# An up projection over the whole TensorE array, zero-padded table products, and bias rows in free strips

## The reference

```
x = x + L0(x)      # per-entry low-rank weight:  x @ (U V)
x = x + L1(x)      # styled linear layer with demodulation and clamp
# L2, an adapter; dg, db, ug, ub come from the entry's condition (256 -> 64 -> 256 features)
down = einsum('bsd,bdh->bsh', x, down_project * dg + db)
up   = einsum('bsh,bhd->bsd', relu(down), up_project * ug[b] + ub[b])
x = x + (up + x)
# L3: layer norms of x with gain and shift looked up by class ids, then a two-layer net
h = LN(LN(x, pw[id]), cp[id]);  t = LN(x, tm[id]);  s = LN(x, ms[id])
m, n, r = x + per-entry rows;   cat = [w0 h, w1 t, w2 m, w3 n, w4 r, w5 s]
x = x + LN(silu(cat @ int_W1 + int_b1) @ int_W2 + int_b2)
```

## Time and profile before

| | |
|---|---|
| median of three runs | 538.83 us (535.41 to 541.04) |
| span of the profiled execution, first to last instruction | 530.8 us |
| median less that span | 8.0 us |
| mean granted TensorE clock | 0.988 of full speed |
| busy: TensorE, VectorE, ScalarE, GpSimd | 497.0, 406.6, 326.3, 390.5 us |

### The profile page before, as it was taken

How to read it: one execution, slowest core, us unless ns; L and a number is a source line. 1 busy time by engine, 2 the same in 40 slices (tenths; PEclk the granted TensorE clock), 3 DMA queues, 4 the chain that set the end, 5 groups by cost and what they waited for, 6 DMA issues and landing times.

```text
span 530.8 us, 9969 instructions
## 1 busy us (share of the span) xinstructions
PE 497.0 (94%) x3454; PEld 352.4 (66%) x3454; DVE 406.6 (77%) x707; ACT 326.3 (61%) x622; POOL 390.5 (74%) x367
## 2 busy tenths in 40 slices
PE   2987988989999999999999999999999999999993
PEld 2953654757777676767676767677676767687682
DVE  1858877758888787879787878788787978786753
ACT  4574647346666576756765757567575767656822
POOL 6468798788787879697877787787878693777321
PEclk9999998999999999999999999999999999999997
DMA  8887714625252262708070716244352613104102
GB/s 297 244 297 201 198 40 101 159 81 123 81 120 84 48 194 39 202 5 237 0 219 23 190 52 162 80 114 128 78 165 41 203 33 89 48 17 145 40 2 79
DMA packets 35639, 61.85 MB, mean 117 GB/s; under 512 B 6002, under 2 KB 18062, under 8 KB 35229
## 3 DMA queue, kind: packets, MB, share of 16 engines
q1 hardware_dynamic: 29404, 44.03, 30.2%
q0 software_dynamic: 5344, 16.87, 11.0%
q10 hardware_dynamic: 864, 0.61, 0.4%
HBM read 52.63 MB, written 8.87 MB: 116 GB/s over the span
## 4 chain that ended last, share of the span: by engine, by line
PE 78%; DVE 10%; issue 4%; DMA 4%; ACT 2%; POOL 1%; DVEq 0%; SPq 0%; POOLq 0%; ACTq 0%
PE ps_c L906 13%; PE ps_c L908 11%; PE ps_c L907 11%; PE ps_d L952 10%; PE ps_a L982 6%; PE ps_d L966 5%; PE ps_a L994 3%; PE ps_a L1000 3%; PE ps_b L1000 3%; DMA set_wdec<-in_nets_rows 3%; PE ps_b L939 3%; DVE tm_t_l L1439 3%; DMA set_wdec<-in_W_dec 1%; PE ps_a L488 1%; PE ps_b L923 1%
## 5 line engine op out<-in xcount | busy, mean ns | idle before, releaser
L1509 POOL DMA_INDIRECT pw_rows<-in_pw,gidx x64 | 63.4, 990 | 17.9 <-issue 17.4
L952 PE MATMUL ps_d<-xm_t,l_w 128*128 128x512 f32 x128 | 58.9, 603 | 1.2 <-POOL xm_t L1518 0.8
L1208 ACT ACTIVATE h<-h,nb_h,rstd_h 128x256 f32<-128x256 f32 x64 | 33.3, 591 | 33.8 <-POOL nb_h L1533 33.8
L1518 POOL TENSOR_TENSOR xm_t<-x_t,style 128x1024 f32<-128x1024 f32 x16 | 30.5, 1905 | 26.4 <-DVE x_t L1343 26.4
L1548 POOL TENSOR_TENSOR h<-xhat,pw_rows 128x1024 f32<-128x1024 f32 x16 | 37.9, 2369 | 7.6 <-ACT xhat L1208 7.1
L952 PEld LDWEIGHTS ps_d<-xm_t,l_w 128*128 128x128 f32 x128 | 23.1, 190 | 25.9 <-issue 24.2
L1567 POOL TENSOR_TENSOR w_up<-up_rep,ugub 128x1024 f32<-128x1024 f32 x16 | 37.9, 2367 | 2.2 <-issue 2.0
L1553 POOL TENSOR_TENSOR h<-h,pw_rows 128x1024 f32<-128x1024 f32 x16 | 38.3, 2392 | 1.3
L1569 POOL TENSOR_TENSOR w_up<-w_up,ugub 128x1024 f32<-128x1024 f32 x16 | 38.2, 2387 | 1.3
L906 PE MATMUL ps_b<-w_h,act_t_l 128*128 128x256 f32 x128 | 37.7, 295 | 0.4 <-DVE act_t_l L1452 0.4
L1239 ACT ACTIVATE tm_t_h<-ps_a 128x1024 fp32r<-128x1024 f32 x16 | 16.4, 1027 | 34.8 <-DVE ps_a L1415 34.8
(11 more groups left out here) (247 smaller groups left out, 1527.0 us busy)
## 6 DMA issues: line engine op xcount, KB each, us to landing
ugub<-ugub_scratch SPq DMA_DIRECT2D x32, 512.0 KB
x_t<-in_x_t SPq DMA_DIRECT2D x16, 512.0 KB
out<-y_out SPq DMA_DIRECT2D x15, 512.0 KB
set_wdec<-in_W_dec SPq DMA_DIRECT2D x2, 1920.0 KB, 9.7
set_wdec<-in_int_W SPq DMA_DIRECT2D x1, 1536.0 KB, 10.6
set_wdec<-in_nets_rows SPq DMA_DIRECT2D x1, 1152.0 KB, 13.6
pw_rows<-in_pw,gidx POOLq DMA_INDIRECT x64
set_wdec<-in_nets_W SPq DMA_DIRECT2D x1, 768.0 KB, 4.9
```

The lines of the kernel that those rows point to most:

```text
L952: m = eng.matmul(ps_l1[:, o, :], l1_w[:, k, o * P:(o + 1) * P], xm_t[:, k, :], start=k == 0, stop=k == KB - 1)
L1208: m = eng.activation(out[:, j, :], src[:, j, :], ACT.Identity, bias=nb[k][:, j:j + 1], scale=rstd[k][:, j:j + 1])
L1509: eng.indirect_dma_start(pw_rows[c.ring][:, j, :], None, t["pw"], bass.IndirectOffsetOnAxis(ap=gidx[c.ring][:, j:j + 1], axis=0)).then_inc ...
```

## The change

- The up projection becomes eight matmuls of 128 weight rows and 128 columns. `act_dn` is [128, 4, 2, 64] and zero off its two diagonal blocks (rows of e hold columns of e), so that one full-array product gives both entries. `act_relu` writes the two blocks in two instructions, `v_x3sum` adds in one.
- The ms scale product and the shift product use all 128 rows of tables and one-hot, with zeros where nothing belongs; their two matmuls are therefore full-array ones. The shift table's two blocks lie side by side in 256 columns, its DMA per chunk is one instead of two.
- The bias rows of the second layer move to partitions 32 and 96, next to the tm product at 0 and 64.
- Seven tiles are zeroed at the start on VectorE instead of one, and their first users wait for that; `act_shift` copies the shift table in one instruction instead of two and the bias rows in two instead of one.

```
-        shift = [sb(f"shift{r}", [P, P], BF16) for r in range(2)]
+        shift = [sb(f"shift{r}", [P, D], BF16) for r in range(2)]
-        act_dn = sb("act_dn", [P, CT * S])
+        act_dn = sb("act_dn", [P, CT, 2, S])
-        pads = (ubias_p,)
+        pads = (ubias_p[:, :], act_dn[:, :, :, :], onehot[0][:, :], onehot[1][:, :], shift[0][:, :], shift[1][:, :], gain_tab[:, 2 * D:3 * D],)
...
 def load_entry
-                for lo in (0, STRIP):
-                    eng.dma_start(onehot[n][lo + CLS:lo + CLS + BRW, :], t["entry_rows"]).then_inc(d_oh, 16)
+                eng.dma_start(onehot[n][CLS:CLS + BRW, :], t["entry_rows"]).then_inc(d_oh, 16)
...
 def v_classes
-            for k in range(KB):
-                m = eng.tensor_copy(shift[0][k * STRIP:k * STRIP + CLS, :], src[:, k * P:(k + 1) * P])
-            m.then_inc(v_cls, 1)
+            eng.tensor_copy(shift[0][0:CLS, :], src).then_inc(v_cls, 1)
...
 def act_shift
-            for k in range(KB):
-                rows = slice(k * STRIP, k * STRIP + CLS)
-                eng.activation(shift[1][rows, :], shift[0][rows, :], ACT.Copy)
-            eng.wait_ge(g_b2, 2)
-            eng.activation(b2_row[STRIP:STRIP + PIECES, :], b2_row[0:PIECES, :], ACT.Copy).then_inc(c_shift, 1)
+            eng.activation(shift[1][0:CLS, :], shift[0][0:CLS, :], ACT.Copy)
+            eng.wait_ge(g_b2, 2)
+            for k in range(KB):
+                lo = k * STRIP + RP
+                m = eng.activation(b2_row[lo:lo + PIECES, :], b2_row[0:PIECES, :], ACT.Copy)
+            m.then_inc(c_shift, 1)
...
 def load_shift
-            for k in range(KB):
-                lo = k * STRIP + CLS
-                eng.dma_start(shift[c.ring][lo:lo + BRW, :], one(rowc_d, c)[:, k * P:(k + 1) * P]).then_inc(s_row[c.ring], 16)
+            eng.dma_start(shift[c.ring][CLS:CLS + BRW, :], one(rowc_d, c)).then_inc(s_row[c.ring], 16)
...
 def pe_up
-                    for e in range(2):
-                        rows, m = slice(e * HID, (e + 1) * HID), k * CT + j
-                        m = eng.matmul(ps_up[:, e, m * S:(m + 1) * S], w_up[rows, j, k * P:(k + 1) * P],
-                                       act_dn[rows, j * S:(j + 1) * S], start=True, stop=True)
+                    m = eng.matmul(ps_up[:, k, j * P:(j + 1) * P], w_up[:, j, k * P:(k + 1) * P],
+                                   act_dn[:, j, :, :], start=True, stop=True)
...
 def pe_ms
-            gains(eng, ps_ms, c, 2 * D).then_inc(p_ms, 1)
+            for k in range(KB):
+                m = eng.matmul(ps_ms[:, k, :], gain_tab[:, 2 * D + k * P:2 * D + (k + 1) * P], onehot[c.ring][:, :],
+                               start=True, stop=True)
+            m.then_inc(p_ms, 1)
...
 def shift_bank
-            rows = slice(o * STRIP, o * STRIP + CLS + BRW)
-            eng.matmul(ps_w1[:, o, :], shift[c.ring][rows, :], onehot[c.ring][rows, :], start=True, stop=False)
+            eng.matmul(ps_w1[:, o, :], shift[c.ring][:, o * P:(o + 1) * P], onehot[c.ring][:, :], start=True, stop=False)
...
 def pe_w2
-                rows = slice(k * STRIP, k * STRIP + PIECES)
+                rows = slice(k * STRIP + RP, k * STRIP + RP + PIECES)
                 eng.matmul(ps_y[:, k, :], ones[rows, :], b2_row[rows, :], start=True, stop=False)
...
 def act_relu
-            eng.activation(act_dn[:, :], dn[:, :], ACT.Relu).then_inc(a_relu, 1)
+            for e in range(2):
+                rows = slice(e * HID, (e + 1) * HID)
+                m = eng.activation(act_dn[rows, :, e, :], dn[rows, :].rearrange("p (j s) -> p j s", s=S), ACT.Relu)
+            m.then_inc(a_relu, 1)
...
 def v_x3sum
-            for e in range(2):
-                m = eng.scalar_tensor_tensor(halves(x3_t[:, :, :])[:, e], halves(x2_t[:, :, :])[:, e], 2.0,
-                                             ps_up[:, e, :].rearrange("p (m s) -> p m s", s=S), ALU.mult, ALU.add)
-            m.then_inc(v_x3t, 1)
+            eng.scalar_tensor_tensor(x3_t[:, :, :], x2_t[:, :, :], 2.0, ps_up[:, :, :],
+                                     ALU.mult, ALU.add).then_inc(v_x3t, 1)
```

More of the change, by code:

```diff
@@ L569, in v_pads @@
             for tile in pads:
-                eng.memset(tile[:, :], 0.0).then_inc(z_pad, 1)
+                eng.memset(tile, 0.0).then_inc(z_pad, 1)
         def v_ubias(eng, c):
@@ L672, in v_gains @@
             pick(eng, v_link, gain_tab[0:CLS, :], tab[1][:, :], *(p[:, :] for p in tab_p))
-            eng.scalar_tensor_tensor(gain_tab[STRIP:STRIP + CLS, :], tab_p[2][:, :], masks[:, 2:3], tab[1][:, :],
-                                     ALU.mult, ALU.add).then_inc(v_pick, 1)
+            eng.scalar_tensor_tensor(gain_tab[STRIP:STRIP + CLS, 0:2 * D], tab_p[2][:, 0:2 * D], masks[:, 2:3],
+                                     tab[1][:, 0:2 * D], ALU.mult, ALU.add).then_inc(v_pick, 1)
         def v_w1sum(eng, c):
@@ L913, in pe_t @@
             if first(c):
-                eng.wait_ge(d_oh, 80)
+                eng.wait_ge(d_oh, 48)
                 eng.wait_ge(v_ub, 1)
@@ L1070, in pe_shift @@
             wait(eng, a_oh, c.n + 1)
-            wait(eng, s_row[c.ring], 32 * (c.half + 1))
+            wait(eng, s_row[c.ring], 16 * (c.half + 1))
             shift_bank(eng, c, 0)
@@ L1184, in act_relu @@
         def act_relu(eng, c):
+            if first(c):
+                eng.wait_ge(z_pad, len(pads))
             wait(eng, v_dn, c.n + 1)
             wait(eng, p_up, c.n)
-            eng.activation(act_dn[:, :], dn[:, :], ACT.Relu).then_inc(a_relu, 1)
+            for e in range(2):
+                rows = slice(e * HID, (e + 1) * HID)
+                m = eng.activation(act_dn[rows, :, e, :], dn[rows, :].rearrange("p (j s) -> p j s", s=S), ACT.Relu)
+            m.then_inc(a_relu, 1)
         def act_x3h(eng, c):
@@ L1389, in v_x3sum @@
             wait(eng, v_x3l, c.n)
-            def halves(ap):
-                return ap.rearrange("p k (j e s) -> p e (k j) s", e=2, s=S)
-            for e in range(2):
-                m = eng.scalar_tensor_tensor(halves(x3_t[:, :, :])[:, e], halves(x2_t[:, :, :])[:, e], 2.0,
-                                             ps_up[:, e, :].rearrange("p (m s) -> p m s", s=S), ALU.mult, ALU.add)
-            m.then_inc(v_x3t, 1)
+            eng.scalar_tensor_tensor(x3_t[:, :, :], x2_t[:, :, :], 2.0, ps_up[:, :, :],
+                                     ALU.mult, ALU.add).then_inc(v_x3t, 1)
         def stats(eng, c, k, src, s_bn, s_mv):
```

## The result

| | before | after |
|---|---|---|
| median | 537.04 us (530.18 to 541.45, 20 runs) | 525.29 us (523.71 to 531.13, 20 runs) |
| ratio | | 0.9845, 95% interval 0.9819 to 0.9871 |
| profiled execution: span, granted clock | 530.8 us, 0.988 | 523.4 us, 0.995 |

By the ratio the kernel is faster by 1.55% (1.3 to 1.8%), some 8.3 us; the two medians stand 11.75 us apart, a ratio of 0.978. The ratio leaves out executions over 1.5% above the fastest of their kernel as slow ones, which by the list on record are 8 of the 20 of before and none of after, so it counts less of the spread of before than the medians do.

A forecast was written before the change was run, and what follows sets the result against it. TensorE, busy 28.18 of 28.40 us per period, bounds the kernel, with waits on two chains. -4.8 (up) - 1.6 (end) + 0.65 (start) = -5.7 us off the 538.8 median gives 533.1; range from just under 529.1 to 538.8.

The forecast's parts named there:

- The up projection: TensorE, chunks 2 to 15: 2.26 us between w1 records instead of 2.60, saving 0.34 us each, 4.8 us in all.
- The rival in which load and stream don't overlap: Full-array up: weight loads not hidden under the stream, 1.8 us more less 0.3, 14 times, 560 us; chance 0.03.
- Gaps between strips and the full array: Around up: full-array form removes 0.09 us at entry, 0.20 at exit; rival that gaps stay: 543.3 us, chance 0.04.
- Bias rows, ms and shift in the loop: Loop pieces where chains from tm and to x2 decide: bias rows 0.22 us earlier, ms and shift about 0.09, worth nothing.
- stretch the tm pair: Bias rows beside tm: four strips at once might stretch tm by up to 0.07 us, 0.7 over ten periods; left out.
- The end: Last chunks: bias rows 0.2, shifts 0.6 and 0.5, ms and shift pairs 0.35, together 1.6 us saved.
- relu: ScalarE, two instructions: about 0.33 us more each, covered in the loop, uncovered at the first two ups, plus 0.65 us.
- l1's room: Loop, l1 behind styled x1: 1.1 us of room, 0.34 used, so l1 less than 0.8 us behind xm afterwards.
- The start: Before the loop: relu's split delays the first two ups, plus 0.65 us; up saves nothing between these two.
- what lies around the span: Profiled execution's own time not given, so the saving on the 530.8 us span was taken off the median, 538.8 us.
- The rival that the loop and the end gained more than counted: Chains from tm and to x2 shorten too: bias rows, ms and shift add 0.40 us for ten periods, 529.1; chance 0.18.

The follow-up runs named there:

- kernel 4: Only the bias rows of the second layer moved to the strips at 32 and 96, against the kernel before: 535.25 us, ratio 1.0021.
- kernel 3: The changed kernel with up, relu and x3sum as before (full-array shift and ms, moved bias rows, zeroed tiles kept): 531.12 us, ratio 0.9944 to before.
- kernel 9: The kernel before with half of the tm product with transposed xhat left out, shortening the chain from tm: 533.72 us, ratio 0.9963.
- kernel 10: The changed kernel with half of the tm product with transposed xhat left out: 519.56 us, ratio 0.9731 to before, only 2 runs.
- Kernel 2: The kernel before with the block-diagonal up projection alone, plus relu in two instructions and x3sum in one: 524.2 us, ratio 0.9832, 6 runs.
- kernel 1: The kernel before run once more, without any edit: 534.35 us, ratio 1.0014.
- kernel 11: The kernel before with 18 more filler products in the start, strips kept in up: 530.3 us, ratio 0.994.
- kernel 12: The changed kernel with the same 18 more filler products in the start: 524.47 us, ratio 0.9843 to before, 6 runs.
- kernel 5: The kernel before with the full-array up projection in chunks 0 and 1 only, strips in chunks 2 to 15: 530.83 us, ratio 0.995.
- kernel 6: The kernel before with the full-array up projection in chunks 2 to 15, strips in chunks 0 and 1: 528.49 us, ratio 0.9893.
- kernel 8: The changed kernel with the tm product ahead of the down projection in TensorE's loop order: 529.61 us, ratio 0.9926 to before.

## Why the prediction was wrong

The direction was right, the time too high by 7.8 us and outside the range. 1.8 of it is the common value of before, 537.04 us in all 20 runs against 538.83 in the first three. The other 6.0 are gain that the sum doesn't have: 11.75 us between the medians (8.3 by the ratio), where 5.7 were forecast. Point by point:

- **The up projection: right.** 16 records, 1.95 us, the pitch of the set-up block, 2.25 us from record to record where 2.26 was worked out. The period fell by 0.33 us where 0.34 was. The rival in which load and stream don't overlap is out. Here the Trainium skill ("TensorE: Matmul & The Clock Gate", what overlaps and what doesn't) would have full-array f32 products lose the cover of their weight loads, and the trace disagrees: 16 records in 1.95 us.
- **Gaps between strips and the full array: right**, up and the single shift products show them gone. "TensorEngine Tiling (Array Packing)" of the Trainium skill, key properties, says that a change of mode drains the array; the trace agrees, with 0.33 us against 0.24 at the entry of up.
- **Bias rows, ms and shift in the loop: right.** They start as forecast, and the chains from tm (3.97 us) and from l1 swallow it; kernel 4 shows it for the bias rows, kernel 3 for all, kernels 9 and 10 give its size, 0.20 us. Four strips did not stretch the tm pair: from tm to the end of tm_t_l are 3.97 us against 3.98. By the figure of the Trainium skill ("TensorE: Matmul & The Clock Gate", measured speedup against the span model: 3.07 times for four row tiles) up to 0.07 us more were possible, an estimate; the trace doesn't show them.
- **The end: nearly.** -2.1 us where 1.6, and 3 times 0.34 for the ups of the last three chunks that lie in it, make 2.6. Kernel 2 gives 1.0 for the ups, kernel 3 1.4 for the rest; their sum is 2.4, and together they give 0.3 less.
- **relu: the delay right in sum, the price wrong.** From the first down projection to the second up projection are 28.13 us instead of 27.46, +0.67 where 0.65 was forecast; it is 0.47 at the first up and 0.17 at the second, not 0.33 twice, so the sum is in part luck. And kernel 7, which splits relu and does nothing else, costs 2.6 to 4.1 us.
- **l1's room: wrong, without harm.** I had it at less than 0.8 us behind xm; in the loop it is 0.88 to 1.07, as x1 comes sooner too.
- **The start, and what lies around the span: here the prediction failed.** "The profiled execution's own time is not given, so I take the difference off the median" and "what lies around the span is therefore taken as the difference to the median" put 8.0 us outside the kernel's work. Only 1.8 are. The rest was span: the profiled execution, at a clock of 0.988, is above all twelve of kernel 1 (0.974 to 0.987), and of the 87 executions of before that ran beside the kernels only 8 have as much (0.969 to 0.992, median 0.979). The profiled ones among those of lower clock have longer stretches of half clock in the start and longer spans. So the step that failed is the start's term, "+0.65": it was nearly the right sum of waits at full clock (0.46 between kernels 11 and 12), and had the wrong sign for this kernel, as it put the clock's part at nothing. None of the rivals had the clock in it, although the 0.988 stood in the table and the page's clock row had its 8 in the start.

What the runs show of this term: taking the strips out of the first two up projections gives about 3 us (kernel 5); leaving them in costs 3.3 us of what the up projection gives alone, by the ratios 0.9893 and 0.9832 (kernels 6 and 2, the second from six runs only). Fillers around the strips give 3.2 us as well (kernel 11), and add nothing clear once the strips are out (kernel 12). With the clocks alike the change is worth 5.8 us, as summed. By their ratios kernels 5 and 6, which share the up projection between them, make 2.7 + 5.7 = 8.4 us, close to the 9.0 of kernel 2. The 1.4 us of the end (kernel 3) should come on top, and the ratio of the whole doesn't show them; the medians have room for them.

The mean clock alone doesn't order everything: at 0.991 seven executions of after have spans of 523.4 to 527.1 us (median 526.0), and the two of before at 0.991 and 0.992 have 528.7 and 529.7, some 3 us more and not 5.7. The start spreads for other reasons too, as the 47.4 to 50.6 us at its first down projection show. The rival that the loop and the end gained more than counted falls with kernels 2 and 3; that it is chance, with kernels 5 to 7 and 11, with 12 runs each: 5 and 11 raise the median clock to 0.992 and 0.9945, kernel 6 leaves it at 0.981 with 14 of the 16 ups changed, and kernel 7 has 0.978, with no run above 0.981, where its rival had it rise.

Where the clock halves in the start, by small windows of the profiled executions (start, length in us; all of them also have half clock in the last 3 to 6 us, and kernels 1 and 5 a stretch of 3.4 us around 500), and how long the stretch from the first down projection to the up projection of chunk 2 takes (us from start to start):

| kernel | up of chunks 0 and 1 starts | half clock | first down projection to up of chunk 2 |
|---|---|---|---|
| before | 54.86, 77.39, strips | 80.8 for 3.4; 91.1 for 3.4 | 52.50 |
| 1 | 53.13, 77.32, strips | 55.8 for 3.4; 79.6 for 10.2 | 55.86 |
| 3 | 52.34, 74.87, strips | 78.0 for 6.8; 91.7 for 3.4 | 54.40 |
| 4 | 55.11, 80.91, strips | 56.4 for 6.8; 83.7 for 6.8; 97.3 for 3.4 | 57.55 |
| 6 | 53.02, 78.81, strips | 53.7 for 6.8; 81.0 for 10.2 | 57.44 |
| 7 | 54.23, 78.58, strips | 56.7 for 3.4; 80.6 for 10.2; 97.6 for 3.4 | 58.00 |
| 9 | 54.23, 80.02, strips | 55.0 for 6.8; 82.3 for 10.2 | 57.47 |
| 11 | 54.30, 76.86, strips, fillers | none | 51.21 |
| 2 | 55.24, 82.41, full array | 50.9 for 13.7 | 56.07 |
| 8 | 56.52, 79.25, full array | 50.4 for 3.4 | 52.17 |
| 5, 10, 12 and after | full array | none | 51.66 to 51.71 |

The last column goes with the one before it: 51.2 to 51.7 us without half clock, 55.9 and 56.1 with 13.6 us of it (strips and full arrays), 57.4 to 58.0 with 17. So a microsecond at half clock costs this stretch about 0.35 us there; in before, with two short stretches late in it, 1.3 us for 6.8. That gives an estimate for the medians: a mean clock of 0.979 over some 532 us (before, the 87 executions) is 22 us at half clock, one of 0.994 over 523 us (after) is 6, and 16 us less at 0.35 are 5.6 us, about the 6.0 that the sum lacked.

Open stays why strips in particular let the clock fall. What the table shows is when: without fillers, in each execution with strips a fall begins in or within 1.5 us behind one of the first two up projections or behind both, and none begins there where they are full-array ones. But the falls at 91.1, 91.7, 97.3 and 97.6 us stand at neither of the two, and kernels 2 and 8 have a fall ahead of chunk 0's up, so the form of this stage is not the only cause. Kernel 3, with strips in up and full arrays elsewhere, lies between in its clock. Each row is one execution.

## What to carry to other kernels

Read the granted clock ahead of every sum: where it is under 1.00, find the stretches of half clock by small windows, and count what the change does to TensorE's work around them; here that was a third of the gain by the ratio, half of it by the medians. Never take the difference between a profiled span and a median for overhead: it may be a profiled run that was luckier than the median. And when time is taken out of an engine that is 99% busy, first find the waits in its period: only what lies in a piece without one counts, and a kernel with the waiting chain cut short tells how much is hidden there.

## What the runs showed of the hardware

- The granted clock in the start depends on the form of a few products. From 48 to 98 us it is 1.00 in kernel 5's profiled execution and 0.83 in kernel 6's; over the whole execution kernel 5 has a median of 0.992 and kernel 6 of 0.981 (12 runs each), before has 0.979 and after 0.994. In this start 17 us at half clock cost about 6 us of time. At half clock a block of 16 full-array f32 records takes 3.75 instead of 1.95 us.
- In f32, a pair of 64-row strips with 64 columns has the same pitch, 0.11 us, as one full-array record with 128 columns: here strips gained nothing on TensorE. By l1's rate (8 records of 512 columns in 3.70 us) 64 columns would take up to 0.06 us, an estimate, so something else sets the pace; both forms load 128 columns of weights for each record.
- Going from full array to strips and back costs 0.09 us at the entry (0.33 against 0.24) and 0.2 us at the exit (0.54 against 0.34).
- Four strips at partitions 0, 32, 64 and 96 (two of 24 rows, two of 3, 512 bf16 columns each) start within 0.01 us of one another, with no stretch that these traces show.
- The time around the span is 1.8 or 1.9 us in each of the 20 runs of after and in each of the other kernels' runs.
